# Second modulation on turned tiles, first normalizations on VectorE, twelve row places, another order for the last tiles

## Chip, cores, metric

One NeuronCore of a Trainium2 chip runs the whole kernel in one launch. The metric is the device time of an execution in microseconds. Each figure of the profile comes from one profiled execution.

## What is computed

Two batches of 2048 tokens, 128 channels. `mod` gives six vectors of 128 per batch. The first half is a gated linear recurrence, the second a mixture of eight experts of which each token takes two.

```python
sa, ca, ga, sb, cb, gb = (mod[:, 0], mod[:, 1], mod[:, 2], mod[:, 3], mod[:, 4], mod[:, 5])
h = _layernorm(x, axis=-1) * (1 + ca) + sa
x = x + ga * _L0_attn_ref(h, ...)      # two sigmoid gates, a = exp(log_a), y = scan(a, b)
h = _layernorm(x, axis=-1) * (1 + cb) + sb
x = x + gb * _L0_ffn_ref(h, ...)
# ffn: logits = silu(x @ rw1 + rb1) @ rw2 + rb2; top 2 of 8, softmax;
#      out += we[:, None] * (silu(x @ w1[e] + b1[e]) @ w2[e] + b2[e])
```

## The kernel before

The 4096 tokens are eight groups of 512 (four tiles of 128 rows); groups 0 to 3 are batch 0, 4 to 7 batch 1. Everything is float32.

For each group g, in the names of the order lists: `stats1` (mean and variance, VectorE), `rstd1` (GpSimd, power -0.5), `norm1` (GpSimd for groups 0 to 2, VectorE for the rest), `turn_x` (TensorE turns rows to channels), `modulate` (ScalarE, 1 + ca and sa as per-partition scale and bias), `gates` (TensorE), `tanh`, `decay` (exp), `clamp`, `mult` (sqrt) on ScalarE, `input` and `scan` on VectorE, `turn_y` back, `resid` (adds x, statistics of the second norm), `rstd2` on GpSimd for groups 0 to 3 or `root` on VectorE for 4 to 7, and `norm2`: eight instructions that subtract the mean, multiply by 1 + cb, multiply by rs and add sb, with cb and sb spread over all partitions by `modrow` and `rowsA`. Then `turn_h`, `copy` (ScalarE), four `router` products with four `silu`, `logits`, `lgc`, `sum`, `top2`, `share`, `rank` and `place`, which gives each token's two slots in DRAM.

`send` (GpSimd): 64 indirect DMAs, eight for each group, write the normalized rows with weight and target row to `sorted_rows`, each expert's rows together. They wait for `place` of the group and for a doubling DMA that SP issues after `norm2`. Each expert's rows end in a padding block, written by eight DMAs of SP once `late_table` has given the offsets (`pad_i`).

The expert stage works through 39 tiles of 256 rows of one expert. `early_table` (after group 3 has its slots) lists the first nine tiles, all of batch 0; `late_table` and `table_row` (after group 7) the other 30. Per tile: SP loads the rows (`xr`), TensorE turns them (`tx`, bank 1), VectorE copies them out (`xT`) and copies the expert's first weights to a pair of buffers (`w1`), TensorE runs layer1 (`l1`), ScalarE `hid` (silu), VectorE `w2`, TensorE layer2 (`l2`, bank 7), ScalarE `yb`, TensorE turns back (`ty`, bank 1), VectorE scales (`sc`), GpSimd scatters two halves to `expert_out` (`scat`). `tx` and `ty` share bank 1 in a fixed turn. Rows and results have ten places each (`U`), so the load of tile s waits for the scatter of tile s - 10.

Up to tile 10 every engine follows its list in `PLAN` (instructions joined with + alternate); then come a loop over 20 tiles (`ROUNDS * U`) and a static rest with `step`. In the rest, `SUMS` says in which step VectorE adds the two expert results of a group (`combine`, three instructions). SP's queue in order: input loads, eight doublings, nine tile loads (after `s_tab` 1 and the sends of batch 0), eight paddings, tile loads from 9 on (after `s_tab` 2, padding, all sends), loads of results, stores. At the end four DMAs of SP fetch group 7's results in halves. `keep_warm` issues eleven matmuls of ident beside the first small products.

## Time and profile before

| | |
|---|---|
| time, median of 3 runs | 288.79 us (288.6 to 292.12) |
| profiled execution | 288.09 us, span 286.2 us |
| TensorE busy | 248.1 us, 87% |
| VectorE busy | 188.4 us, 66% |
| ScalarE busy | 166.5 us, 58% |
| GpSimd busy | 171.6 us, 60% |
| mean granted TensorE clock | 0.956 |

The span runs from the first to the last instruction. Engines are PE (TensorE; PEld its weight loads), DVE (VectorE), ACT (ScalarE), POOL (GpSimd) and SP; SPq is the queue on which SP issues DMAs. L1205 is line 1205 of the kernel. In a timeline row the bracket gives the idle time ahead of the instruction and what ended it. A float32 matmul shows as two records.

### The profile page before, as it was taken

The page shows a single profiled execution, that of the slowest core. Times are in us where ns is not written, and L with a number is a line of the kernel's source. Part 1 is how long each engine was busy: PE and PEld are TensorE (multiplying, and loading weights), DVE is VectorE, ACT ScalarE, POOL GpSimd, SP SyncE. Part 2 cuts the span into 40 slices and gives each one's busy share as a digit, 9 for nine tenths or more (in the row PEclk, how much of TensorE's full clock was granted, in tenths as well). Part 3 has the DMA queues.
Part 4 walks back from the last instruction along what each step waited for, and adds up shares of the span by engine and source line. Part 5 has one row for each costly group of instructions (what it writes and reads, how often), then busy time and mean ns, then how long its engine had stood idle before and what let it go on. Part 6 is the DMA issues. An engine that isn't in the chain of part 4 may idle for free.

```text
span 286.2 us, 4950 instructions
## 1 busy us (share of the span) xinstructions
PE 248.1 (87%) x1179; PEld 178.0 (62%) x1179; DVE 188.4 (66%) x750; ACT 166.5 (58%) x322; POOL 171.6 (60%) x192
## 2 busy tenths in 40 slices
PE   7767759997599798999999999999999999989910
PEld 6424334444144245687878888888888888868700
DVE  3959999999999987576444444444444446866533
ACT  4189979999785355545555555555555556445300
POOL 4996211267777757777777777644554445645650
PEclk9997979999779799999999999999999999999995
DMA  7993011121131226413533333222217822280505
GB/s 222 308 333 117 19 40 38 37 75 50 55 121 48 89 82 157 114 47 115 149 84 85 111 101 109 57 75 75 74 46 214 221 72 74 84 256 4 161 0 147
DMA packets 45365, 30.51 MB, mean 107 GB/s; under 512 B 5085, under 2 KB 41999, under 8 KB 45342
## 3 DMA queue, kind: packets, MB, share of 16 engines
q1 hardware_dynamic: 40432, 21.75, 27.9%
q0 software_dynamic: 4544, 8.47, 9.0%
q8 instruction: 8, 0.13, 0.2%
q14 instruction: 15, 0.12, 0.2%
q10 hardware_dynamic: 366, 0.04, 0.1%
HBM read 16.39 MB, written 12.67 MB: 102 GB/s over the span
## 4 chain that ended last, share of the span: by engine, by line
PE 40%; POOL 27%; issue 14%; DVE 12%; DMA 4%; POOLq 1%; DVEq 0%; SPq 0%; ACT 0%
POOL sorted_rows L550 21%; PE bank L1218 18%; PE bank L1205 18%; POOL shared L514 3%; PE bank L1226 3%; PE bank L1194 2%; DVE st L698 2%; DMA expert_out<-shared,tx 2%; POOL rs L506 1%; DVE shared L718 1%; POOL expert_out L559 1%; DVE tx L792 1%; DMA xs<-in_L_attn_x_dram 1%; DVE xs L803 1%; DMA tx<-sorted_rows 1%
## 5 line engine op out<-in xcount | busy, mean ns | idle before, releaser
L559 POOL DMA_INDIRECT expert_out<-shared,tx x78 | 80.4, 1031 | 52.9 <-DVE shared L1012 37.4
L657 ACT ACTIVATE hT<-bank,w_t 128x256 f32<-128x256 f32 x156 | 65.4, 470 | 29.3 <-PE bank L1205 28.3
L550 POOL DMA_INDIRECT sorted_rows<-rows,sloti x64 | 63.9, 999 | 27.2 <-issue 18.3
L1205 PE MATMUL bank<-xT,w_t 128*128 128x256 f32 x312 | 74.1, 380 | 0.1
L1218 PE MATMUL bank<-hT,w_t 128*128 128x256 f32 x312 | 74.1, 380 | 0.0
L1205 PEld LDWEIGHTS bank<-xT,w_t 128*128 128x128 f32 x312 | 56.3, 190 | 6.8 <-DVE w_t L995 0.7
L1218 PEld LDWEIGHTS bank<-hT,w_t 128*128 128x128 f32 x312 | 56.2, 190 | 6.2
L666 ACT ACTIVATE yT<-bank,w_t 128x256 f32<-128x256 f32 x39 | 18.4, 473 | 47.6 <-PE bank L1218 47.6
L1134 PE MATMUL bank<-h2T,rw_s 128*128 128x512 f32 x64 | 36.8, 677 | 1.7 <-ACT qv L644 1.4
L986 DVE COPY xT<-bank 128x256 f32<-128x256 f32 x39 | 16.5, 422 | 23.6 <-PE bank L1194 23.6
L1012 DVE TENSOR_TENSOR shared<-bank,tx 128x256 f32<-128x256 f32 x39 | 16.5, 423 | 21.3 <-PE bank L1226 21.2
L995 DVE COPY w_t<-w_s 128x516 f32 x39 | 17.2, 442 | 16.7 <-issue 15.9
L1004 DVE COPY w_t<-w_s 128x513 f32 x39 | 17.3, 443 | 15.3 <-issue 14.4
L1134 PEld LDWEIGHTS bank<-h2T,rw_s 128*128 128x128 f32 x64 | 10.8, 205 | 14.4 <-issue 5.9
L698 DVE BATCH_NORM_STATS2 st<-xs 128x6 f32<-128x128 f32 x64 | 15.7, 282 | 4.2 <-DMA xs<-in_L_attn_x_dram 4.1
L1226 PE MATMUL bank<-ident,yT 128*128 128x128 f32 x78 | 15.2, 276 | 2.5 <-ACT yT L666 1.1
L1194 PE MATMUL bank<-ident,tx 128*128 128x128 f32 x78 | 15.2, 276 | 1.8 <-DMA tx<-sorted_rows 1.3
L1226 PEld LDWEIGHTS bank<-ident,yT 128*128 128x128 f32 x78 | 10.3, 141 | 8.3 <-issue 3.3
L1194 PEld LDWEIGHTS bank<-ident,tx 128*128 128x128 f32 x78 | 10.4, 141 | 7.7 <-DMA tx<-sorted_rows 2.3
L644 ACT ACTIVATE qv<-bank,smallbT 128x512 f32<-128x512 f32 x16 | 10.8, 686 | 6.3 <-PE bank L1134 6.2
L506 POOL TENSOR_TENSOR rs<-ve,half_neg 128x4 f32<-128x4 f32 x8 | 9.3, 1164 | 8.0 <-DVE ve L705 8.0
L542 POOL TENSOR_TENSOR rs<-ve,half_neg 128x4 f32<-128x4 f32 x4 | 4.1, 1035 | 15.7 <-DVE ve L705 15.7
(194 smaller groups left out, 328.9 us busy)
## 6 DMA issues: line engine op xcount, KB each, us to landing
tx<-sorted_rows SPq DMA_DIRECT2D x39, 130.0 KB, 2.2
w_s<-in_L_ffn_w_dram SPq DMA_DIRECT2D x16, 256.0 KB, 6.1
xs<-in_L_attn_x_dram SPq DMA_DIRECT2D x8, 256.0 KB, 5.2
rows<-rows SPq DMA_DIRECT2D x8, 256.0 KB, 2.6
av<-expert_out SPq DMA_DIRECT2D x8, 256.0 KB, 3.7
qv<-expert_out SPq DMA_DIRECT2D x6, 256.0 KB, 5.0
expert_out<-shared,tx POOLq DMA_INDIRECT x78, 2.3
sorted_rows<-padr SPq DMA_DIRECT2D x9, 130.0 KB, 3.0
```

Source lines behind the costliest of these rows:

```text
L550: p.indirect_dma_start(sorted_rows[:, :], bass.IndirectOffsetOnAxis(ap=sloti[:, k, t:t + 1], axis=0), rows[:, t, k, :], None).then_inc(s_d ...
L559: p.indirect_dma_start(expert_out[:, :], bass.IndirectOffsetOnAxis(ap=xr_i[:, s % U, n, D + 1:D + 2], axis=0), yo[:, s % U, n, :], None, b ...
L657: ins = nc.scalar.activation(hsT[:, u % 2, h, :], bank[4 + q][:, (h % 2) * SL:(h % 2 + 1) * SL], ACT.Silu, bias=w1_t[:, u % 2, HID + h:HID ...
L666: nc.scalar.activation(yT[:, u % 2, :], bank[7][:, 0:SL], ACT.Identity, bias=w2_t[:, u % 2, HC * D:W2E]).then_inc(s_yT_e, 1)
L698: ins = v.bn_stats(st[:, t, :], xs[:, t, :])
L995: v.tensor_copy(w1_t[:, u % 2, :], w1_s[:, bass.ds(e * WE, WE)]).then_inc(s_w1t, 1)
L1004: v.tensor_copy(w2_t[:, u % 2, :], w2_s[:, bass.ds(e * W2E, W2E)]).then_inc(s_w2t, 1)
L1134: t.matmul(bank[2 + n % 2][:, :], rw1_s[:, h * P:(h + 1) * P], h2T[:, g % 2, :], start=True, stop=True).then_inc(s_rl1, 1)
L1194: ins = t.transpose(bank[1][:, n * P:(n + 1) * P], xr[:, u, n, 0:D], ident[:, :])
L1205: ins = t.matmul(bank[4 + h // 2][:, (h % 2) * SL:(h % 2 + 1) * SL], w1_t[:, u % 2, h * P:(h + 1) * P], xT[:, u % 2, :], start=True, stop= ...
L1218: ins = t.matmul(bank[7][:, 0:SL], w2_t[:, u % 2, h * D:(h + 1) * D], hsT[:, u % 2, h, :], start=(h == 0), stop=(h == HC - 1))
L1226: ins = t.transpose(bank[1][:, n * P:(n + 1) * P], yT[:, u % 2, n * P:(n + 1) * P], ident[:, :])
```

## The change

- `norm2` only subtracts the mean and multiplies by rs (four instructions). 1 + cb and sb are applied after the turn, where they are per-partition values: for the router in `copy` on ScalarE, for the experts in `take_x`. `mod2` and `mods2` compute these columns; `modrow` and `rowsA` keep only gb.
- A tile from 9 on can hold rows of both batches. A third row of the table gives its split; `take_x` then writes all columns with batch 0's values and after that the columns from the split on with batch 1's.
- `w2` moves from VectorE to ScalarE. `norm1` is VectorE's for all groups. `keep_warm` is gone.
- Rows and results have twelve places; tiles 0 and 1 use places 10 and 11, and the lists go up to tile 11.
- The last tiles: layer2 of 37 has bank 2 and stands ahead of layer1 of 38, and the last bias, turn, scale and scatter go by halves. Group 7's result loads are issued half by SP, half by ScalarE.
- All lists are in another order.

```diff
     U = 10
-    FIRST = 11
+    FIRST = 12
+    SLOTS = 12
-    POOLED = 3
             "tensor": """
+                turnc:0 mod:0 turn_x:0 mod2:0 gates:0 turn_x:1 turn_x:2 gates:1 gates:2 turn_x:3 turn_x:4 gates:3
+                turn_x:5 turn_y:0 gates:4 turnb:0 turn_y:1 gates:5 modrow:0 turn_h:0 turn_x:6 router:0 turn_h:1
+                router:1 turn_y:2 gates:6 router:2 router:3 router:4 turn_y:3 logits:0 router:5 router:6 sum:0
+                turn_h:2 turn_x:7 router:7 rank:0 router:8 turn_y:4 router:9 logits:1 router:10 router:11 turn_h:3
+                sum:1 logits:2 rank:1 sum:2 router:12 turn_h:4 router:13 gates:7 router:14 rank:2 turn_y:5 router:15
+                turn_y:6 router:16 logits:3 router:17 sum:3 turn_h:5 router:18 router:19 rank:3 router:20 logits:4
+                turn_h:6 count:0 sum:4 router:21 turn_y:7 router:22 router:23 router:24 rank:4 router:25 router:26
+                logits:5 router:27 turn_h:7 sum:5 logits:6 router:28 router:29 rank:5 router:30 router:31 tx:0 sum:6
+                tx:1 l1:0 tx:2 logits:7 rank:6 l1:1 l2:0 tx:3 l1:2 sum:7 ty:0 lev:0 l2:1 tx:4 l1:3 ty:1 l2:2 rank:7
+                tx:5 l1:4 ty:2 l2:3 tx:6 count:1 l1:5 ty:3 l2:4 tx:7 l1:6 ty:4 l2:5 tturn:0 tx:8 l1:7 ty:5 l2:6 l1:8
+                ty:6 l2:7 tx:9 tx:10 l1:9 ty:7 l2:8 tx:11 l1:10 ty:8 l2:9 tx:12 l1:11 ty:9 l2:10""",
             "vector": """
...
-                norm2:4 place:2 norm2:5 scan:6 scan:7+top2:3 resid:6 place:3 resid:7+root:6 norm2:6 top2:4+root:7
...
-                w1:2 xT:2 xT:3 w1:3 w2:1 rowsB:0 sc:0 w2:2 top2:7 xT:4 w1:4 place:7 w2:3 sc:1 w1:5 xT:5 w2:4 table2:0
-                sc:2 w1:6 xT:6 sc:3 xT:7 w2:5 w1:7 w2:6 sc:4 w2:7 xT:8 table3:0 sc:5 w1:8 w1:9 sc:6 w2:8 xT:9 w2:9
-                w1:10 xT:10 sc:7 xT:11 w1:11 sc:8 w2:10""",
+                stats1:0 setup:0 stats1:1+norm1:0 stats1:2+mods:0 norm1:1+soft:0 norm1:2 stats1:3 input:0 stats1:4
+                norm1:3+stats1:5 csilb:0 norm1:4 input:1 mods2:0 norm1:5 scan:0 scan:1 stats1:6 input:2
+                resid:0+stats1:7 resid:1 input:3 colsb:0 norm2:0 norm2:1 norm1:6 scan:2 scan:3 resid:2+consts:0
+                input:4 scan:4+rowsA:0 norm2:2 resid:3+norm1:7 top2:0 place:0 norm2:3 resid:4 root:4 norm2:4 top2:1
+                place:1 input:5 input:6 top2:2 scan:5 scan:6 resid:5+place:2 resid:6+root:5 norm2:5 top2:3+root:6
+                norm2:6 input:7 place:3 scan:7 table1:0+top2:4 resid:7 root:7 norm2:7 place:4 top2:5 w1:0 place:5 xT:0
+                xT:1 top2:6 w1:1 xT:2 w1:2 place:6 w1:3 xT:3 table1b:0 sc:0 xT:4 top2:7 w1:4 sc:1 xT:5 w1:5 place:7
+                sc:2 w1:6 xT:6 table1c:0 sc:3 w1:7 xT:7 table2:0+rowsB:0 sc:4 w1:8 xT:8 table3:0 w1:9 sc:5 sc:6 xT:9
+                xT:10 sc:7 w1:10 w1:11 xT:11 sc:8 xT:12 w1:12 sc:9""",
...
-                hid:4 yb:3 hid:5 yb:4 hid:6 yb:5 hid:7 yb:6 hid:8 yb:7 hid:9 yb:8 hid:10""",
+                csil:0 esp:0 modulate:0 tanh:0 modulate:1 decay:0 modulate:2 clamp:0 tanh:1 decay:1 mult:0 clamp:1
+                modulate:3 mult:1 tanh:2 modulate:4 tanh:3 decay:2 modulate:5 clamp:2 tanh:4 decay:3 decay:4 tanh:5
+                mult:2 copy:0 clamp:3 mult:3 modulate:6 clamp:4 mult:4 silu:0 silu:1 copy:1 silu:2 silu:3 silu:4
+                decay:5 lgc:0 silu:5 silu:6 copy:2 share:0 silu:7 tanh:6 modulate:7 clamp:5 silu:8 silu:9 lgc:1
+                silu:10 silu:11 decay:6 lgc:2 share:1 copy:3 clamp:6 mult:5 mult:6 silu:12 copy:4 silu:13 share:2
+                silu:14 tanh:7 silu:15 decay:7 lgc:3 silu:16 clamp:7 silu:17 copy:5 silu:18 share:3 silu:19 mult:7
+                lgc:4 silu:20 silu:21 copy:6 silu:22 silu:23 silu:24 share:4 silu:25 lgc:5 silu:26 silu:27 copy:7
+                silu:28 share:5 lgc:6 silu:29 silu:30 silu:31 hid:0 w2:0 share:6 hid:1 w2:1 yb:0 lgc:7 w2:2 hid:2 yb:1
...
+        def out_bank(s):
+            return bank[2] if static(s) and s == TILES - 2 else bank[7]
         SUMS = {FIRST + ROUNDS * U: 0, FIRST + ROUNDS * U + 1: 1, FIRST + ROUNDS * U + 2: 2,
-                FIRST + ROUNDS * U + 3: 3, MID + 13: 4, FIVE + 6: 5, TILES + 1: 6}
+                FIRST + ROUNDS * U + 3: 3, FIRST + ROUNDS * U + 4: 4, TILES - 1: 5, TILES + 1: 6}
...
-            return (s - u) // U + 1
+            if static(s) and s < SLOTS:
+                return 1
+            return (s - u) // U + 1 if u >= SLOTS - U else (s - u - U) // U + 1
...
+        def slot(s):
+            return U + s if s < SLOTS - U else s % U
...
+        def load_last(eng, k):
+            for half, done in ((0, s_y01[NG - 1]), (1, s_y7b)):
+                at = k * TOK + (NG - 1) * G + half * G // 2
+                eng.dma_start(y01[NG - 1][:, k, 2 * half:2 * half + 2, :], expert_out[at:at + G // 2, :]
+                              .rearrange("(n p) d -> p n d", p=P)).then_inc(done, 16)
...
-                if not (static(s) and s < U):
+                if not (static(s) and s < SLOTS):
...
-                if s * HALVES * ROW + HALVES * ROW > GPB * G and s * HALVES * ROW <= GPB * G:
+                if s == 0:
...
-            def ln1_norm(g):
-                pool.wait_ge(s_rstd1, g + 1)
...
-                for j in range(GT):
-                    t = g * GT + j
-                    ins = p.tensor_scalar(xn[:, g % 2, j, :], xs[:, t, :], mv1[:, t, 0:1], rs1[:, t:t + 1],
-                                          ALU.subtract, ALU.mult)
-                ins.then_inc(s_xnp, 1)
...
                 for n in range(HALVES):
+                    if s == TILES - 1 and n:
+                        pool.wait_ge(s_yo, s + 1 + n)
...
-                nc.scalar.copy(h2T[:, g % 2, :], turn_bank("turn_h", g)[:, :]).then_inc(s_h2T, 1)
+                if g == 0:
+                    act.wait_ge(s_modok, 2)
+                b = g // GPB
+                nc.scalar.activation(h2T[:, g % 2, :], turn_bank("turn_h", g)[:, :], ACT.Identity,
+                                     bias=modc[:, 3, b:b + 1], scale=gac[:, 3, b:b + 1]).then_inc(s_h2T, 1)
...
+            def weights2(s, u):
+                if static(s) and s == 0:
+                    act.wait_ge(s_tab, 1)
+                if static(s) and s == EARLY:
+                    act.wait_ge(s_tab, 2)
+                e = act.value_load(tab[0:1, 1, bass.ds(s, 1)], min_val=0, max_val=NE - 1)
+                if static(s) and s == 0:
+                    act.wait_ge(s_w2, 16 * NE)
+                    act.wait_ge(s_constd, 1)
+                if not (static(s) and s < 2):
+                    act.wait_ge(s_yT_e, s - 1)
+                nc.scalar.copy(w2_t[:, u % 2, :], w2_s[:, bass.ds(e * W2E, W2E)]).then_inc(s_w2t, 1)
...
+            def bias_last(s, u):
+                act.wait_ge(s_l2, s + 1)
+                act.wait_ge(s_yturn, s - 1)
+                for n in range(HALVES):
+                    nc.scalar.activation(yT[:, u % 2, n * P:(n + 1) * P], out_bank(s)[:, n * P:(n + 1) * P],
+                                         ACT.Identity, bias=w2_t[:, u % 2, HC * D:W2E]).then_inc(s_yT_e, 1)
             def step(s, u):
+                if static(s) and s >= TILES - 1:
+                    if s == TILES - 1:
+                        bias_out(s - 2, step_slot(s, u, -2))
+                        weights2(s, u)
+                        bias_out(s - 1, step_slot(s, u, -1))
+                        hidden(s, u)
+                        bias_last(s, u)
+                    return
...
                     hidden(s, u)
+                    weights2(s, u)
...
+            landed(act, TILES - 1)
+            load_last(act, 1)
...
+            def mod_columns2(_):
+                dve.wait_ge(s_modc, 2)
+                yield from link(v.tensor_copy(modc[:, 3:5, :], bank[6][:, 3 * B:5 * B].rearrange("p (i b) -> p i b", b=B)))
+                v.tensor_scalar(gac[:, 3, :], modc[:, 4, :], 1.0, None, ALU.add).then_inc(s_modok, 1)
...
             def ln2_norm(g):
-                b = g // GPB
                 for j in range(GT):
                     t = g * GT + j
-                    ins = v.scalar_tensor_tensor(rows[:, t, 0, 0:D], xs[:, t, :], mv2[:, t, 0:1], cbB[:, b, :],
-                                                 ALU.subtract, ALU.mult)
-                    if j < GT - 1:
-                        yield
-                yield from link(ins)
-                for j in range(GT):
-                    t = g * GT + j
-                    ins = v.scalar_tensor_tensor(rows[:, t, 0, 0:D], rows[:, t, 0, 0:D], rs2[:, t:t + 1],
-                                                 sbB[:, b, :], ALU.mult, ALU.add)
+                    ins = v.tensor_scalar(rows[:, t, 0, 0:D], xs[:, t, :], mv2[:, t, 0:1], rs2[:, t:t + 1],
+                                          ALU.subtract, ALU.mult)
...
                 for b in range(B):
                     m = bank[6 + b]
-                    v.tensor_copy(sbB[:, b, :], m[:, 0:D])
+                    v.tensor_scalar(gbS[:, b, :], m[:, 0:D], 0.0, 2.0, ALU.is_ge, ALU.mult)
                     yield
-                    v.tensor_scalar(cbB[:, b, :], m[:, D:2 * D], 1.0, None, ALU.add)
-                    yield
-                    v.tensor_scalar(gbS[:, b, :], m[:, 2 * D:3 * D], 0.0, 2.0, ALU.is_ge, ALU.mult)
-                    yield
-                    ins = v.tensor_copy(gbB[:, b, :], m[:, 2 * D:3 * D])
+                    ins = v.tensor_copy(gbB[:, b, :], m[:, 0:D])
...
+                by_level = val2[:, 2, :].rearrange("p (l e) -> p l e", l=LEVELS)
+                v.tensor_copy(row_0[:, 2:3], first[:, 0:1])
...
                 dve.wait_ge(s_tturn, 1)
-                v.tensor_scalar(tab[:, :, EARLY:TILES], table_bank().rearrange("p (k s) -> p k s", k=2),
-                                float(NE * REG), None, ALU.min).then_inc(s_tab, 1)
+                turned = table_bank().rearrange("p (k s) -> p k s", k=3)
+                v.tensor_scalar(tab[:, 0:2, EARLY:TILES], turned[:, 0:2, :], float(NE * REG), None, ALU.min)
+                v.tensor_copy(split[:, :], turned[:, 2, :]).then_inc(s_split, 1)
+                dve.wait_ge(s_split, 1)
+                v.tensor_tensor(split[:, :], split[:, :], turned[:, 0, :], ALU.subtract).then_inc(s_split, 1)
+                dve.wait_ge(s_split, 2)
+                v.tensor_scalar(tab[:, 2, EARLY:TILES], split[:, :], 0.0, float(SL), ALU.max, ALU.min).then_inc(s_tab, 1)
                 dve.wait_ge(s_tab, 2)
             def expert_of(s):
                 return dve.value_load(tab[0:1, 1, bass.ds(s, 1)], min_val=0, max_val=NE - 1)
             def take_x(s, u):
+                early = static(s) and s < EARLY
+                if not early:
+                    k = dve.value_load(tab[0:1, 2, bass.ds(s, 1)], min_val=0, max_val=SL)
                 dve.wait_ge(s_txp, s + 1)
                 if not (static(s) and s < 2):
                     dve.wait_ge(s_l1, 2 * (s - 1))
-                v.tensor_copy(xT[:, u % 2, :], bank[1][:, 0:SL]).then_inc(s_xT, 1)
+                if static(s) and s == 0:
+                    dve.wait_ge(s_modok, 2)
+                v.tensor_scalar(xT[:, u % 2, 0:SL], bank[1][:, 0:SL], gac[:, 3, 0:1], modc[:, 3, 0:1],
+                                ALU.mult, ALU.add).then_inc(s_xT if early else s_xa, 1)
+                if not early:
+                    dve.wait_ge(s_xa, s - EARLY + 1)
+                    v.tensor_scalar(xT[:, u % 2, bass.ds(k, SL)], bank[1][:, bass.ds(k, SL)], gac[:, 3, 1:2],
+                                    modc[:, 3, 1:2], ALU.mult, ALU.add).then_inc(s_xT, 1)
...
-            def weights2(s, u):
-                e = expert_of(s)
...
+            def scale_last(s, u):
+                for n in range(HALVES):
+                    dve.wait_ge(s_yturn, s + 1 + n)
+                    v.tensor_tensor(yo[:, u, n, :], bank[1 - n][:, 0:P], xr[:, u, n, D:D + 1].to_broadcast([P, D]),
+                                    ALU.mult).then_inc(s_yo, 1)
...
-            def keep_warm(n):
-                if n == 0:
-                    pe.wait_ge(s_ident, 1)
-                for _ in range((4, 4, 3)[n]):
-                    t.matmul(bank[4][:, 0:P], ident[:, :], ident[:, :], start=True, stop=True)
...
+            def modulation2(_):
+                pe.wait_ge(s_modok, 1)
+                for i in range(3, 5):
+                    ins = t.matmul(bank[6][:, i * B:(i + 1) * B], wmod_s[:, i * D:(i + 1) * D], csil[:, :],
+                                   start=True, stop=True)
+                ins.then_inc(s_modc, 1)
...
-                    ins = t.matmul(bank[6 + b][:, 0:3 * D], csil_b[:, b, :], wmod_s[:, 3 * D:6 * D],
-                                   start=True, stop=True)
+                    ins = t.matmul(bank[6 + b][:, 0:D], csil_b[:, b, :], wmod_s[:, 5 * D:6 * D], start=True, stop=True)
...
             def xn_transpose(g):
-                if g < POOLED:
-                    pe.wait_ge(s_xnp, g + 1)
-                else:
-                    pe.wait_ge(s_xn, g - POOLED + 1)
+                pe.wait_ge(s_xn, g + 1)
...
+            def layer2(s, u, between=None):
                 pe.wait_ge(s_w2t, s + 1)
-                pe.wait_ge(s_hs, 2 * (s + 1))
+                if not (static(s) and s == TILES - 1):
+                    pe.wait_ge(s_hs, 2 * (s + 1))
                 if static(s) and s < 1:
                     pe.wait_ge(s_tab, 1)
+                elif static(s) and s >= TILES - 2:
+                    pe.wait_ge(s_yT_e, TILES - 2 if s == TILES - 1 else TILES - 3)
                 else:
                     pe.wait_ge(s_yT_e, s)
                 for h in range(HC):
-                    ins = t.matmul(bank[7][:, 0:SL], w2_t[:, u % 2, h * D:(h + 1) * D], hsT[:, u % 2, h, :],
+                    if static(s) and s == TILES - 1 and h % 2 == 0:
+                        pe.wait_ge(s_hs, 2 * s + h // 2 + 1)
+                    ins = t.matmul(out_bank(s)[:, 0:SL], w2_t[:, u % 2, h * D:(h + 1) * D], hsT[:, u % 2, h, :],
                                    start=(h == 0), stop=(h == HC - 1))
+                    if h == 1 and between:
+                        between()
                 ins.then_inc(s_l2, 1)
...
+            def turn_last(s, u):
+                for n in range(HALVES):
+                    pe.wait_ge(s_yT_e, s + 1 + n)
+                    if n == 0:
+                        wait_tile_bank(pe, "ty", s)
+                    t.transpose(bank[1 - n][:, 0:P], yT[:, u % 2, n * P:(n + 1) * P], ident[:, :]).then_inc(s_yturn, 1)
...
+                if static(s) and s >= TILES - 1:
+                    if s == TILES - 1:
+                        layer2(s - 1, step_slot(s, u, -1), lambda: turn_out(s - 2, step_slot(s, u, -2)))
+                        layer1(s, u)
+                        turn_out(s - 1, step_slot(s, u, -1))
+                        layer2(s, u)
+                        turn_last(s, u)
+                    return
```

## Rows read from the trace of the kernel before

**Rows 1.** The page's 40 slices of 7.155 us, busy tenths: TensorE, VectorE, ScalarE.
```profile
PE   7767759997599798999999999999999999989910
DVE  3959999999999987576444444444444446866533
ACT  4189979999785355545555555555555556445300
```
**Rows 2.** The chain of waits, 143 to 155 us: start, us, what.
```profile
143.89 1.00 POOL expert_out L559
...
148.28 2.31 DMA tx<-sorted_rows
...
151.07 1.73 PE bank L1205 x8
...
154.97 1.73 PE bank L1205 x8
```
**Rows 3.** Stretches: length, then each engine's busy us, granted clock, DMA share, GB/s.
```profile
34.00:38.70 4.70, 0.00 (x0) 0.00 (x0) 4.67 (x21) 4.06 (x6) 0.46 (x1) 1.00 0.00 0
38.70:43.00 4.30, 4.27 (x12) 2.62 (x13) 4.23 (x6) 3.39 (x5) 0.58 (x1) 0.60 0.24 67
...
151.00:266.00 115.00, 113.79 (x580) 97.58 (x579) 58.50 (x132) 61.86 (x144) 67.11 (x66) 1.00 0.37 103
```
**Rows 4.** VectorE's timeline: a first normalization, and the padding offsets.
```profile
20.47 1.11 DVE L718 TENSOR_SCALAR shared<-xs,mv,rs 128x128 f32<-128x128 f32 x4 [2.47 <-POOL rs L506]
...
131.10 0.14 DVE L960 CAST pad_i<-bank 1x8 int32<-1x8 f32 x1
```
**Rows 5.** Groups of instructions, VectorE: busy us, mean ns, idle before.
```profile
L1004 DVE COPY w_t<-w_s 128x513 f32 x39 | 17.3, 443 | 15.3 <-issue 14.4 <-ACT yT L666 0.9
...
L986 DVE COPY xT<-bank 128x256 f32<-128x256 f32 x39 | 16.5, 422 | 23.6 <-PE bank L1194 23.6
...
L823 DVE SCALAR_TENSOR_TENSOR rows<-rows,rs,sbB 128x128 f32<-128x128 f32 x32 | 9.4, 343 | 0.2
...
L718 DVE TENSOR_SCALAR shared<-xs,mv,rs 128x128 f32<-128x128 f32 x20 | 5.9, 335 | 2.5 <-POOL rs L506 2.5
```
**Rows 6.** ScalarE's timeline at a change of tables.
```profile
22.39 1.28 ACT L620 ACT_TABLE_LOAD   x1
23.68 0.63 ACT L620 ACTIVATE qv<-qv 128x512 f32<-128x512 f32 x1
```
**Rows 7.** TensorE's timeline: first gate, tile 0's layer1, tile 7's row turn.
```profile
11.46 2.05 PE L1110 MATMUL bank<-hT,wx_bd 128*128 128x512 f32 x2 [0.96 <-ACT hT L592]
...
111.48 1.97 PE L1205 MATMUL bank<-xT,w_t 128*128 128x256 f32 x8
...
137.47 0.38 PE L1194 MATMUL bank<-ident,tx 128*128 128x128 f32 x2
```
**Rows 8.** GpSimd's timeline: sends 1, 32 and 64.
```profile
58.18 1.38 POOL L550 DMA_INDIRECT sorted_rows<-rows,sloti  x1 [5.73 <-DVE sloti L864]
...
99.86 0.96 POOL L550 DMA_INDIRECT sorted_rows<-rows,sloti  x1 [0.31 <-issue]
...
142.63 0.96 POOL L550 DMA_INDIRECT sorted_rows<-rows,sloti  x1 [0.31 <-issue]
```
**Rows 9.** SP's timeline, 99 to 148 us: start, us of issuing, queue.
```profile
106.08 10.05 SPq L411 DMA_DIRECT2D tx<-sorted_rows  x9
132.01 8.39 SPq L400 DMA_DIRECT2D sorted_rows<-padr  x8
145.72 0.39 SPq L411 DMA_DIRECT2D tx<-sorted_rows  x1
```
**Rows 10.** The page's DMA issues: KB each, median us to landing.
```profile
sorted_rows<-padr SPq DMA_DIRECT2D x9, 130.0 KB, 3.0
```
**Rows 11.** Timeline of the tail: PE's weight load of tile 37's turn, SP's last loads.
```profile
270.37 0.20 PEld L1226 LDWEIGHTS bank<-ident,yT 128*128 128x128 f32 x2 [0.97 <-ACT yT L666]
...
278.19 1.91 SPq L465 DMA_DIRECT2D qv<-expert_out  x4
```

158 lines of the change are left out of this document (67 added, 91 removed).

## Prediction

> **What bounds the kernel now.** I read the page's slices first [rows 1]. From slice 2 to 14 (7 to 107 us) VectorE stands at 8 or 9 and PE mostly at 5 to 9; from slice 17 on PE stands at 9 and VectorE at 4 to 6. Next the chain of waits [rows 2]: before it comes to these rows it runs through GpSimd's 64 indirect sends, one after the other; then come the scatter of tile 0, its landing, the load of tile 10, and from 151.07 us layers of TensorE back to back, 3.90 us from one tile's first layer to the next tile's. A stretch view confirms it: 113.8 of the 115 us from 151 to 266 are PE's, while VectorE is 51% and ScalarE 54% busy [rows 3]. So three things set the end: how early the tile stage starts, what holds it at tiles 9 and 10 (the first that need all sends), and the tail.
>
> **The start, up to the first send.** VectorE's order up to place:0 is nearly a sum of its own work; after the gap that ends at 20.47 [rows 4] it has none worth naming until the first send's slots are ready near 57.8. Ahead of place:0 the change adds three first normalizations (L718 at 335 ns, overlapping, four in 1.03: 3.1 in all), scan:4 (two instructions, 1.9) and mods2 (two tiny ones, 0.35). It takes off input:5 (0.6), half of rowsA (four instructions of 0.2, 0.8), and L823 [rows 5], the second instruction of norm2, for groups 0 to 2. Four L823 fill 1.15 us alone, but two of the three sets stand between statistics and partly fill gaps: 0.66 + 0.66 + 1.2 = 2.5. Less interleaving costs some 0.6. Net +2.0. Against this stands the gap of 2.47 us at 20.47 [rows 4], where VectorE waited for rs of group 3 because GpSimd, itself normalizing three groups, came late to it; it goes, and a wait of 0.4 for the biases with it. place:0 ends near 57.0: first send 57.3 instead of 58.18, 0.9 earlier.
>
> The cover for this is ScalarE. Counted through its new order it switches tables 15 times instead of 13, once more ahead of share:0 (silu:4, decay:5, silu:5). A switch costs 1.28 us, and the next ACTIVATE starts 0.01 us behind it [rows 6]. By the same durations lgc:0 ends at 52.3, the sums at 53.3, and top2:0 wants them at 53.9: hidden, with 0.6 us to spare. The Trainium skill (ScalarE: Activation LUTs, What ACT_TABLE_LOAD costs) puts a switch at about 2.66 us, a drain included. No such gap stands in these rows, so the measured 1.28 is used; by the page, an estimate, the later table switches would push place:0 some 2 us back and the total to 287.9.
>
> The warm-up matmuls go. They bought nothing: gates:0 still runs at 2.05 us for two records from 11.46 [rows 7], twice the 1.02 of the same pair later, with the warm-up ahead of it. I charge zero. The Trainium skill (TensorE: Matmul & The Clock Gate, Part 1) says that activity ahead releases the half rate, which speaks for keeping them; had it been so here, taking them away could have cost up to 1.9 us of the first gates.
>
> **The sends and tile 0.** 31 intervals from 58.18 to 99.86 make 41.7 us [rows 8]. About 0.5 of that are waits for place:1 and place:2, which now come before their turn: 41.2, so the 32nd send starts at 98.5. The last send starts at 142.63 and the load that waits for all is issued at 145.72, 3.1 us on [rows 8, 9]. The same step puts tile 0's load at 101.6, against 106.08 now [rows 9]. Today it does not wait for sends but for table1 and a register load on SP. In the new order table1 stands before resid:7, root:7 and norm2:7 and ends near 92; norm2:7 ends near 98.5, as five more normalizations are halved (5 x 1.15). place:4 comes at 99.1, which takes most of a hole of 2.1 us ahead of the 33rd send: last send 57.3 + 84.45 - 2.3 = 139.4, seen at 142.5. Layer1:0 starts 5.4 us after its load now (111.48 [rows 7, 9]) and 5.0 then: 106.6.
>
> **What is late next: the padding.** Eight padding DMAs stand on SP's queue ahead of tile 9's load and wait for late_table's pad_i. Now: pad_i 131.10 [rows 4], issues from 132.01 for 8.4 us [rows 9], the last at 140.0, landed a median 3.0 later [rows 10]: 143.0, covered by the sends. The new order holds table2 back behind xT:7. PE from layer1:0 to tx:7: eleven layers of 1.73 (19.0), nine pairs of transposes of 0.22 (2.0), logits:7 and sum:7 (1.8), ranks and counts (0.7), small stalls (0.7): 24.2; the same stretch takes 26.0 now, with router:31 in it (111.48 to 137.47 [rows 7]). So tx:7 at 130.8, pad_i 131.4, first padding +0.9, last +8.0, landed +3.0, register load and issue +0.7: tile 9 is loaded at 144.0, tile 10 at 145.1 (one issue in 1.1 us: nine in 10.05 [rows 9]), it lands 2.3 later [rows 2], and layer1:9 starts at 147.9. Twelve row places do what they are for: tile 10 no longer waits for scatter 0 (143.89 to 148.3 [rows 2]). Today layer1:9 starts at 151.07 in the chain: 3.2 earlier. Bounds: 4.7 if the sends alone decide, 1.0 if table2 slips half a tile.
>
> **The clock after the wait.** PE is through with layer2:7 near 142.4 and then has nothing until 146.3. PE stood still from 34.0 to 38.7, and was then granted a mean 0.60 of its clock until 43, partly 1.2 GHz, partly 2.4 [rows 3]: 0.40 x 4.3 = 1.7 us lost. After a wait of this length I take 1.8; nothing covers it, PE is the bound from there on. Bounds 0 and 2.2. Of the 3.2, 1.4 are left.
>
> **The tile stage.** Per tile VectorE loses the w2 copy (L1004, 0.44) and gains the second column copy (as L986, 0.42, and a short wait for its own first) [rows 5]; a register load goes and one comes. xT is ready 0.5 later, inside layer1's 1.73. ScalarE gains a copy of 513 columns, 0.6 to 0.8 as its forms with 512, and a register load: 3.4 of 3.90 us, hidden. h2T with scale and bias costs up to 0.2 more than as a copy, beside PE. The sums of groups 0 to 4 (2.06 us each on VectorE) now stand in five steps in a row, where VectorE needs 4.4 of 3.90; today such steps cost some 2 us in all. I add 0.3 (0 to 2).
>
> **The tail.** Today the last output transposition but one waits 0.97 us for yT of tile 37, and layer2:38 stands behind it [rows 11]. In the new order layer2:37, in a bank of its own, runs ahead of layer1:38, and layer2:38 follows it with only the second half of hidden to wait for: it ends 0.8 earlier. Half-wide bias, turn and scale bring the scatters 0.4 more forward. The four last loads are issued in turn from 278.19 within 1.91 us [rows 11]; on two queues the first half is complete 0.45 sooner. -1.65 in all (1.0 to 2.2).
>
> **Sum.** -1.4 + 0.3 - 1.65 = -2.75 against the profiled execution's 288.09 us (span 286.2 and 1.9 around it): 285.3. The median of the three runs, 288.79, lies 0.7 above that execution; I say 285.9. 2% of 288.79 (283.0 to 294.6) is about what a measurement of this kernel can tell from no change.
>
> **Rivals.** *The clock holds, or the wait is short* (stalls spread over tiles 0 to 8, or the sends decide): the 1.8 isn't charged and up to 1.5 more comes, 282.6 to 284.3. For it: the order was relieved at both ends; against: the one wait of that length was followed by 0.60 [rows 3]. *ScalarE becomes the bound of the start* (the slower one): place:0, all sends and tile 0 hang one for one on lgc:0, which has 0.6 us of slack. One more late switch and two silus behind it (1.28 + 1.3) make 2.6. The kernel is slower than before once the first send comes after 60.0; at 61.5 it takes 290. For it: ScalarE stands at 7 to 9 in slices 4 to 11; against: at 5 thereafter, so it could catch up [rows 1]. *The two-pass copy and the later table eat the lead*: table2 slips by a tile, the padding lands at 147, layer1:9 starts near 151 and the clock still dips: 287 to 288.8, no change.
>
> **Chances.** Forecast as summed 0.43 (284.5 to 287), clock holds 0.27, table late 0.15, ScalarE bound 0.15. The range leaves out the ends of the first rival and of the slower one: 282.7 to 289.8. Faster than 283.0: 0.17, the better half of the second case and a bit beyond; slower than 294.6: 0.03; within 2%: 0.80.
>
> **What would show it.** First send at 57.3; tile 0's load at 101.6; pad_i near 131.4; tile 9's load right behind the padding's landing, not behind the last send; a hole of some 4 us on PE near 144 and a granted clock near 0.6 after it; then 3.90 us a tile again; from the last layer to the end 12.9 us instead of 13.7. Wrong it is if the first send moves by more than 2 us either way, if PE's hole is under 2 us, or if the steps with sums take over 4.5 us.

## The result, and the profile after

On the chip where both were first timed the changed kernel takes 293.52 us (median of 6, 292.63 to 294.75) and the kernel before 290.51 (median of 6, 288.6 to 292.24): ratio 1.013, 95% interval 1.0085 to 1.0175. That is slower, by 0.85 to 1.75%, and outside the predicted range of 282.7 to 289.8; it stays within the 2% (283.0 to 294.6) that the prediction called no change. A ratio counts, on both sides, only the executions within 1.5% of the fastest of their kernel. The profiled execution takes 292.63 us, span 290.8, mean granted clock 0.935; before it was 288.09, 286.2 and 0.956. The six times of the kernel before fall at 288.6 to 288.9 and at 292.1 to 292.2, and its profile is of a short one: the profiles differ by 4.5 us, the medians by 3.0.

The page's slices (7.27 us each; TensorE, VectorE, ScalarE) answer to [rows 1]: ScalarE has mostly risen by a tenth or two in the tile stage, and TensorE's row has 9 from slice 14 to 35, but for the 3 of slice 20 (145 to 153 us): there TensorE stands still.

```profile
PE   2877679797969899999939999999999999998920
...
DVE  3999987999997946467414355444445554988533
ACT  4199996999978645666633676666676766666500
```

The chain of waits answers to [rows 2]; each line: start, us, what.

```profile
136.04 0.07 DVE pad_i L1003
...
144.25 0.37 SPq L419
...
145.54 2.17 DMA sorted_rows<-padr
...
148.48 2.08 DMA tx<-sorted_rows
...
151.93 0.56 DVE xT L1043
...
153.28 3.41 PE bank L1257 x8
```

GpSimd's sends are gone from this part. In their place stand pad_i, the eight paddings, their landing, the load of tile 9, its turn, and the second pass of its copy. Then tile 9's layer1 takes 3.41 us, twice its usual time. The timelines of GpSimd and SP, which answer to [rows 8] and [rows 9]:

```profile
58.80 1.29 POOL L555 DMA_INDIRECT sorted_rows<-rows,sloti  x1 [1.89 <-DVE sloti L904]
...
142.03 0.95 POOL L555 DMA_INDIRECT sorted_rows<-rows,sloti  x1 [0.30 <-issue]
```

```profile
101.93 0.59 SPq L441 DMA_DIRECT2D rows<-rows  x1
104.06 10.34 SPq L430 DMA_DIRECT2D tx<-sorted_rows  x9
136.84 9.07 SPq L419 DMA_DIRECT2D sorted_rows<-padr  x8
148.48 9.40 SPq L430 DMA_DIRECT2D tx<-sorted_rows  x6
```

The last send starts 0.6 us earlier than before, the padding 4.8 later, and tile 9's load 2.8 later. TensorE's timeline, which answers to [rows 7]: first layer of tile 0, row turn of tile 7, row turns of tiles 9 and 10.

```profile
110.06 1.89 PE L1257 MATMUL bank<-xT,w_t 128*128 128x256 f32 x8
...
135.07 0.38 PE L1246 MATMUL bank<-ident,tx 128*128 128x128 f32 x2
...
150.61 0.56 PE L1246 MATMUL bank<-ident,tx 128*128 128x128 f32 x2 [3.60 <-DMA tx<-sorted_rows]
152.62 0.66 PE L1246 MATMUL bank<-ident,tx 128*128 128x128 f32 x2 [1.45 <-DVE xT L1043]
```

The stretches, which answer to [rows 3]: TensorE has nothing for 3.6 us, is then granted 0.59 of its clock for 8.4 us (a mix of 1.2 and 2.4 GHz), and is full from 159 on.

```profile
147.00:150.60 3.60, 0.02 (x1) 0.00 (x0) 0.00 (x0) 1.71 (x3) 2.82 (x3) 1.00 0.32 92
150.60:159.00 8.40, 6.94 (x23) 5.47 (x24) 3.35 (x7) 1.68 (x4) 6.26 (x8) 0.59 0.46 123
159.00:247.00 88.00, 88.00 (x453) 76.19 (x452) 41.81 (x91) 59.96 (x135) 47.17 (x48) 1.00 0.35 96
```

The costliest groups of the page, which answer to [rows 5]: the copy out of PSUM with a per-partition scale and bias takes 543 ns where the plain one took 422, and each late tile has two of them.

```profile
L1039 DVE TENSOR_SCALAR xT<-bank,gac,modc 128x256 f32<-128x256 f32 x39 | 21.2, 543 | 47.8 <-PE bank L1246 47.1
...
L1043 DVE TENSOR_SCALAR xT<-bank,gac,modc x30 | 16.3, 544 | 4.8 <-DVE xT L1039 2.6
```

The tail, which answers to [rows 11]: the turn of tile 35's output waits for the second pass of xT of tile 38; then ScalarE's yT of tile 36, the scale and the scatters of tile 38, the last loads on two queues.

```profile
269.34 0.41 PE L1285 MATMUL bank<-ident,yT 128*128 128x128 f32 x2 [0.90 <-DVE xT L1043]
...
271.51 0.47 ACT L690 ACTIVATE yT<-bank,w_t 128x256 f32<-128x256 f32 x1 [1.69 <-PE bank L1275]
...
278.10 0.55 DVE L1088 TENSOR_TENSOR shared<-bank,tx 128x128 f32<-128x128 f32 x2 [2.27 <-PE bank L1301]
...
278.81 1.29 POOL L566 DMA_INDIRECT expert_out<-shared,tx  x1 [0.30 <-DVE shared L1088]
...
280.41 1.15 POOL L566 DMA_INDIRECT expert_out<-shared,tx  x1 [0.30 <-issue]
282.96 0.88 SPq L398 DMA_DIRECT2D qv<-expert_out  x2
283.02 0.95 ACTq L398 DMA_DIRECT2D qv<-expert_out  x2
```

Three marks split the difference: ScalarE's first yT of tile 10 (162.65 us before, 167.09 after), that of tile 36 (266.17, 271.51), and the span's end (286.2, 290.8). So **+4.44 up to tile 10, +0.90 from there to tile 36, -0.74 in the tail**: +4.6, which is the difference of the two profiled executions. I use these marks for the experiments too: "stage" is tile 10 to tile 36 (103.52 before, 104.42 after), "end" is tile 36 to the end (20.03, 19.29), "entry" is the start of tile 9's row turn to yT of tile 10 (13.25 before, 149.40 to 162.65; 16.48 after, 150.61 to 167.09).

### The profile page after: what moved, and what is told of

Its sections match the earlier page's. It is cut to its first block, busy times and chain, and to the rows that moved or that the text cites. A ratio compares the mean times of both kernels' runs of the same rounds, so it can differ in the third digit from the quotient of the medians.

```text
span 290.8 us, 5105 instructions
## 1 busy us (share of the span) xinstructions
PE 247.5 (85%) x1162; PEld 178.7 (61%) x1162; DVE 186.7 (64%) x727; ACT 191.4 (66%) x365; POOL 161.3 (55%) x180
## 4 chain that ended last, share of the span: by engine, by line
PE 48%; DVE 33%; issue 5%; DMA 5%; SPq 3%; DVEq 2%; POOL 1%; ACT 1%; POOLq 0%; ACTq 0%
PE bank L1275 17%; PE bank L1257 17%; PE bank L1186 4%; DVE st L740 4%; DVE shared L760 3%; PE bank L1246 3%; DVE rows L863 3%; PE bank L1113 2%; PE bank L1285 2%; DVE xT L1039 2%; DVE mv L745 2%; DVE xs L851 2%; POOL expert_out L566 1%; DMA xs<-in_L_attn_x_dram 1%; SPq L451 1%
## 5 line engine op out<-in xcount | busy, mean ns | idle before, releaser
L566 POOL DMA_INDIRECT expert_out<-shared,tx x78 | 79.5, 1020 | 59.0 <-DVE shared L1061 44.1
L1257 PE MATMUL bank<-xT,w_t 128*128 128x256 f32 x312 | 75.7, 387 | 0.7 <-DVE w_t L1053 0.7
L1257 PEld LDWEIGHTS bank<-xT,w_t 128*128 128x128 f32 x312 | 57.6, 194 | 7.2 <-DVE w_t L1053 0.8
L1275 PEld LDWEIGHTS bank<-hT,w_t 128*128 128x128 f32 x312 | 56.7, 192 | 6.3
L1039 DVE TENSOR_SCALAR xT<-bank,gac,modc 128x256 f32<-128x256 f32 x39 | 21.2, 543 | 47.8 <-PE bank L1246 47.1
L1186 PE MATMUL bank<-h2T,rw_s 128*128 128x512 f32 x64 | 38.5, 708 | 0.2
L684 ACT COPY w_t<-w_s 128x513 f32 x39 | 24.2, 620 | 2.2 <-ACT yT L690 1.0
L1061 DVE TENSOR_TENSOR shared<-bank,tx 128x256 f32<-128x256 f32 x38 | 15.9, 419 | 9.5 <-PE bank L1285 8.6
L1043 DVE TENSOR_SCALAR xT<-bank,gac,modc x30 | 16.3, 544 | 4.8 <-DVE xT L1039 2.6
L1186 PEld LDWEIGHTS bank<-h2T,rw_s 128*128 128x128 f32 x64 | 11.7, 216 | 12.0 <-issue 7.4
```

The costliest lines, as they stand in the source:

```text
L566: p.indirect_dma_start(expert_out[:, :], bass.IndirectOffsetOnAxis(ap=xr_i[:, slot(s), n, D + 1:D + 2], axis=0), yo[:, slot(s), n, :], Non ...
L684: nc.scalar.copy(w2_t[:, u % 2, :], w2_s[:, bass.ds(e * W2E, W2E)]).then_inc(s_w2t, 1)
L1039: v.tensor_scalar(xT[:, u % 2, 0:SL], bank[1][:, 0:SL], gac[:, 3, 0:1], modc[:, 3, 0:1], ALU.mult, ALU.add).then_inc(s_xT if early else s_ ...
L1186: t.matmul(bank[2 + n % 2][:, :], rw1_s[:, h * P:(h + 1) * P], h2T[:, g % 2, :], start=True, stop=True).then_inc(s_rl1, 1)
L1257: ins = t.matmul(bank[4 + h // 2][:, (h % 2) * SL:(h % 2 + 1) * SL], w1_t[:, u % 2, h * P:(h + 1) * P], xT[:, u % 2, 0:SL], start=True, st ...
L1275: ins = t.matmul(out_bank(s)[:, 0:SL], w2_t[:, u % 2, h * D:(h + 1) * D], hsT[:, u % 2, h, :], start=(h == 0), stop=(h == HC - 1))
```

## Experiments

Sixteen kernels in four groups; each group ran on one chip beside the kernel before. The first group's chip gave the kernel before 289.8 us, like the first. The other three gave it 330.8, 332.3 and 332.2 us: there, between 60 and 190 us, engines stop now and then for 2 to 12 us, put down to nothing in the kernel, which no row of the first chip shows. Times of those groups are compared within the group only, and lengths of stretches outside these stalls with the first chip's: the stage of the changed kernel is 104.36 to 104.47 us in its two profiles there and 104.42 on chip one. A longer one of 104.84 in kernel 6 shows how far a single profile can be off.

**1. The table early** (chip one).

```diff
-  ... table1b:0 sc:0 xT:4 ... xT:6 table1c:0 sc:3 w1:7 xT:7 table2:0+rowsB:0 sc:4
+  ... table1b:0 sc:0 table1c:0 xT:4 ... xT:6 table2:0+rowsB:0 sc:3 w1:7 xT:7 sc:4
```

> The changed kernel with table1c right behind sc:0 and table2 right behind xT:6, nothing else. Padding theory (the late table alone makes the hole and with it the dip of the clock): pad_i comes near 131.9 instead of 135.95, the last padding lands some 4 us earlier than now, tile 9 is loaded right behind the landing of the last send at about 145.7 instead of 148.48, TensorE waits about 1 us for it instead of 3.6, its clock stays at 1.00, and layer1:10 starts 4 to 5 us earlier (159.2 to about 154.5): 4.0 to 4.9 us off the changed kernel's time, ratio to the kernel before 0.996 to 1.000. Rival 1 (the clock falls anyway, since the wait is only shortened): 2.7 us off, ratio near 1.004. Rival 2 (the sends or the scatters hold tiles 9 and 10 in any case): under 1 us off, ratio 1.010 or more.

Measured: ratio 0.9989 (0.9952 to 1.0025), against 1.013 for the changed kernel: 1.4%, 4.1 us. SP's and TensorE's timelines:

```profile
101.47 10.56 SPq L430 DMA_DIRECT2D tx<-sorted_rows  x9
131.51 8.48 SPq L419 DMA_DIRECT2D sorted_rows<-padr  x8
144.14 14.55 SPq L430 DMA_DIRECT2D tx<-sorted_rows  x7
...
146.40 0.44 PE L1246 MATMUL bank<-ident,tx 128*128 128x128 f32 x2 [0.69 <-DMA tx<-sorted_rows]
...
148.53 1.89 PE L1257 MATMUL bank<-xT,w_t 128*128 128x256 f32 x8
```

The padding is 5.3 us earlier, 2.1 of it by an earlier first send and 3.3 by the table. Tile 9's load is no longer behind it but behind the landing of the last send (139.59 to 143.34): the row turn of tile 9 waits 0.69 us, and tile 9's layer1 takes its 1.89. Entry is 14.26 us instead of 16.48. Padding theory held. This profiled execution is the shortest of twelve (286.2 us, median 289.88) and had a luckier start, which the next view shows: the changed kernel's own start, here without a half clock. The stretches of this kernel:

```profile
39.00:46.00 7.00, 6.12 (x23) 3.29 (x24) 6.93 (x36) 6.91 (x10) 0.00 (x0) 1.00 0.20 61
144.00:149.00 5.00, 2.87 (x15) 2.06 (x15) 1.77 (x4) 2.36 (x5) 3.78 (x5) 1.00 0.51 132
```

and the same first stretch of the changed kernel:

```profile
39.00:46.00 7.00, 7.00 (x19) 4.24 (x20) 4.58 (x8) 6.43 (x9) 0.00 (x0) 0.57 0.14 43
```

TensorE's and VectorE's timelines in it, first the changed kernel, then this one (both have the same order here):

```profile
39.85 1.92 PE L1186 MATMUL bank<-h2T,rw_s 128*128 128x512 f32 x2
...
44.12 1.03 PE L1113 MATMUL bank<-ident,hT 128*128 128x128 f32 x4
...
45.18 0.69 DVE L851 TENSOR_TENSOR xs<-bank,xs 128x512 f32<-128x512 f32 x1 [2.35 <-PE bank L1113]
```

```profile
39.83 1.02 PE L1186 MATMUL bank<-h2T,rw_s 128*128 128x512 f32 x2
...
41.99 0.60 PE L1113 MATMUL bank<-ident,hT 128*128 128x128 f32 x4
...
43.15 0.67 DVE L851 TENSOR_TENSOR xs<-bank,xs 128x512 f32<-128x512 f32 x1
```

At half clock the two router products and the turn ahead of turn_y:2 take 1.92, 1.91 and 1.03 us instead of 1.02, 1.02 and 0.60, and VectorE waits 2.35 us for it. The first send starts at 56.73 here and at 58.80 in the changed kernel; tile 0 is loaded at 101.47 here, where I had put 101.6.

**2. One copy of xT.** The second pass and its register load are left out: rows of batch 1 from tile 9 on get batch 0's modulation.

```diff
-                if not early:
-                    dve.wait_ge(s_xa, s - EARLY + 1)
-                    v.tensor_scalar(xT[:, u % 2, bass.ds(k, SL)], bank[1][:, bass.ds(k, SL)], ...
```

> The changed kernel with one copy of xT for every tile: leaves out the second pass over the columns that belong to batch 1 (rows of batch 1 from tile 9 on get the modulation of batch 0) and its register load. If the second pass costs what its two places show: tx:10 starts 0.7 us earlier in the hole of tile 9, and in the steps with sums of groups VectorE's work falls by 0.7 us to near 3.7 of 3.9 us, so that the five steps of 4.34 to 4.5 go back to about 3.9: together 2.5 to 3.5 us off the changed kernel, ratio to the kernel before 1.001 to 1.005. If it is hidden as I priced it (0.3 in all): ratio 1.010 or more, steps with sums unchanged.

Measured: ratio 0.9923 (0.9878 to 0.9968). In the profile 3.8 us less than the changed kernel: stage 101.18 instead of 104.42, entry 15.81 instead of 16.48 with the hole (4.16 us) and the half clock still there. The five steps with sums are 3.9 us each instead of 4.34, 4.37, 4.33, 4.54 and 4.98. The second pass isn't hidden. The ratio's 2% is more than the 3.8 us. Two of the twelve executions (285.2 and 285.7 us) ran at a mean clock of 0.95 and 0.956 instead of 0.934 and weigh in it; the median of all twelve, 289.22, lies 4.3 us below the changed kernel's.

**3. turn_y:2 ahead of router:0** on TensorE, the order that makes VectorE wait.

```diff
- turn_x:6 router:0 turn_h:1 router:1 turn_y:2 gates:6
+ turn_x:6 turn_y:2 router:0 turn_h:1 router:1 gates:6
```

> The changed kernel with turn_y:2 ahead of router:0 on TensorE instead of behind router:1, nothing else. If TensorE's order at half clock is what makes VectorE wait 2.35 us at 42.8: that wait falls to under 0.5 us, the first send starts near 57.0 instead of 58.80, and as VectorE has hardly a gap from there to norm2:7, tile 0's load and layer1:0 come 1 to 1.8 us earlier; the end follows by 0.5 to 1.5 us (hole and dip remain, since pad_i hangs on the same stretch), ratio to the kernel before 1.007 to 1.011. Rival: ScalarE's chain to lgc:0 (53.82, then sum:0, top2:0) is next at once, as router:0 comes later by the length of turn_y:2: first send not before 57.9 and tile 0's load moves under 0.5 us, ratio 1.012 to 1.014.

Measured: ratio 1.0129 (1.0088 to 1.0171), no gain. VectorE's wait at 42.8 is gone, but ScalarE's table load ahead of silu:0 starts at 44.05 instead of 42.19, lgc:0 ends 1.73 us later, and the first send comes at 59.92. The rival held: both orders are tied, in profiles with a granted clock of 0.57 and 0.59 from 39 to 46 us.

**4. First normalizations of groups 0 to 2 on GpSimd again**, in the new order.

```diff
- stats1:1+norm1:0 stats1:2+mods:0 norm1:1+soft:0 norm1:2 stats1:3
+ stats1:1 stats1:2+mods:0 soft:0 stats1:3          (and norm1:0 to 2 behind their rstd1 on GpSimd)
```

> The changed kernel with the first normalizations of groups 0 to 2 on GpSimd again, each behind its rstd1, and the rest of every order as changed. My step (VectorE loses 3.1 us of work, but waits 2.47 us for rs of group 3 as the kernel before did): the first send moves by under 1 us either way and the time stays within 1 us of the changed kernel. Rival (VectorE has no slack, and the moved normalizations are what ate the gain of the halved second ones): first send 1.5 us or more earlier, time 1 to 2 us less.

Measured: ratio 1.0267 (1.023 to 1.0305), first send at 62.12. Neither held. TensorE's row turns at 9.59 and 19.54 wait 2.64 and 3.26 us for GpSimd's normalizations, and VectorE 3.99 us at 22.7 for its rs. Having the normalizations on VectorE is worth some 4 us in the order that the change gives, where I had set 3.1 us of added work against a gap of 2.47; the other lists have given up the slack that GpSimd's pace needs.

**5 and 6. Fillers on TensorE** (chip with stalls): 28 idle matmuls ahead of tx:9; 12 behind gates:5 and 10 behind turn_h:0. Neither the changed kernel nor kernel 1 ran on this chip, so the ratios of 5 to 7 say nothing against theirs.

```diff
+                for _ in range((28, 12, 10)[n]):
+                    t.matmul(bank[3 if n == 0 else 2][:, 0:P], ident[:, :], ident[:, :], start=True, stop=True)
```

> The changed kernel with 28 extra 128-column matmuls into an unused bank on TensorE between layer2:7 and the transposition of tile 9, so that TensorE is busy in most of the 3.6 us in which it waited for tile 9. Nothing is left out; 3.0 us of useless work are added where TensorE had nothing to do. If standing still is what brings the dip: granted clock near 1.00 from 150.6 to 159 instead of 0.59, layer1:9 takes 1.89 us instead of 3.62, layer1:10 comes about 2.2 us earlier with tile 9's load unmoved; time 2 to 2.5 us below the changed kernel, ratio to the kernel before 1.004 to 1.007. Rival (the clock falls at that point whatever TensorE does, as it does five times in this kernel): no gain, ratio 1.012 or more.

> The changed kernel with 12 extra 128-column matmuls on TensorE behind gates:5 and 10 behind turn_h:0 (34 to 39 us, where TensorE is 2.07 of 5 us busy). If low activity there is what halves the clock from 39 to 46 (0.57 in the changed kernel's profile, 1.00 in the profile of the kernel with the earlier table, which sent first at 56.73 and not at 58.80): granted clock 1.00 in that stretch, VectorE's wait of 2.35 us for turn_y:2 gone, first send near 56.8, tile 0's load near 101.6, and pad_i 2 us earlier; time 1.5 to 2.5 us below the changed kernel, ratio 1.004 to 1.008. Rival (the dip falls where it likes, or moves to the next stretch): first send anywhere from 56.7 to 59, ratio 1.010 to 1.015.

Measured: 1.0145 (1.0083 to 1.0208) and 0.9949 (0.9908 to 0.999). I had the filler's size wrong: 28 took 6.42 us, 0.23 each. Behind it the clock is 1.00 and layer1:9 takes 1.89, but tile 9 had landed 4.7 us before the filler's end; without it the hole would have been 1.5 us (an estimate: TensorE free at 188.81, load issued at 188.16 and landing 2.2 later). In the second the clock is 1.00 from 39 to 46 us where the first has 0.76, and the first send comes at 57.38 instead of 58.24: the direction held. In two later kernels with the same filler it comes at 57.67 and 58.28, against 57.23 in their control at 0.79. The clock is 1.00 in all three kernels with the filler and in two of the eleven profiles without it that have the same lists up to there; that the filler gains time isn't shown.

**7. A bank for the turned rows** (with the early table): from tile 9 on they go to bank 3, and `ty` waits only for the scale before it.

```diff
+        def x_bank(s):
+            return bank[1] if static(s) and s < EARLY else bank[3]
```

> The kernel with the earlier table, and the transposed rows of tiles 9 and up in a bank of their own (3), so that the output's transposition of a step waits no longer for both passes of xT of the next tile. If the 3.2 us that the second pass costs from the first yT of tile 10 to that of tile 36 (104.42 us with it, 101.18 without) come from the one bank that two transpositions share: that stretch falls to 101.5 to 102.2 us, the five steps with sums to 3.9 to 4.1 us, tx:10 starts right behind tx:9; 2.3 to 3.3 us below the kernel with the earlier table, ratio to the kernel before 0.988 to 0.992. Rival (VectorE's 4.4 us of work in a step with a sum are the bound, whatever bank): the steps stay at 4.3 and only the 0.9 us at step 36 and 1.0 us at tile 10 go, ratio 0.993 to 0.996.

Measured: 0.9945 (0.9907 to 0.9984). The steps with sums are 3.9 us as hoped, stage 101.75, but end is 21.08 instead of 19.3. GpSimd's timeline:

```profile
307.89 0.98 POOL L567 DMA_INDIRECT expert_out<-shared,tx  x1 [2.07 <-DVE shared L1062]
...
310.47 1.07 POOL L567 DMA_INDIRECT expert_out<-shared,tx  x1 [0.30 <-issue]
...
317.47 0.98 POOL L567 DMA_INDIRECT expert_out<-shared,tx  x1 [0.30 <-issue]
```

VectorE needs 4.3 to 4.6 us in a step with a sum and falls behind; the output scales come late, and of the last eight scatters (307.89 to 317.47) the seven behind the first follow each other without a wait. Of the 2.7 us that the stage gains 1.8 are handed to the tail.

**8. Twelve row places alone**, in the kernel before.

```diff
-    FIRST = 11
+    FIRST = 12
+    SLOTS = 12
```

> The kernel before with twelve row places and twelve static steps instead of ten and eleven, nothing else: with it the load of tile 10 waits no longer for the scatter of tile 0. My step: it does what it is for, and alone it is worth only the 0.85 us that the transposition of tile 10 waited for its rows (tile 9's rows come as before): 0.5 to 0.9 us, ratio 0.997 to 0.998. Rival (the whole 3.2 us that I booked for the first tile behind all sends come from here): ratio under 0.993. Other rival (the sums of the first groups start one step later and cost in the tail): ratio 1.000 or more.

Measured: 0.9994 (0.9946 to 1.0042), no difference that this can show. With the places comes another step for the sums of groups 0 to 3, one later, so that five steps with sums stand in a row as in the changed kernel: stage is 104.36 us here against 103.52 before, entry 12.99 against 13.25, end 20.15 against 20.03. The rival of the later sums is seen in the stage, with 0.84 us.

**9 to 12. Control, short filler, combinations** (another chip with stalls). The control is the changed kernel itself.

> The changed kernel once more, as the control that runs on the same chip as the three others: ratio to the kernel before 1.010 to 1.015 as in its own measurement, tile 9's load some 2.7 us behind where the last send's landing would allow it, granted clock about 0.6 from 150.6 to 159.

> The changed kernel with 14 extra 128-column matmuls between layer2:7 and the transposition of tile 9 instead of 28 (28 took 6.42 us and held tile 9 up by some 4.5 us beyond the landing of its rows; 14 take 3.2, less than the wait of 3.6). Standing still as the cause of the dip: clock 1.00 from 150.6 on, layer1:9 in 1.89 us, layer1:10 about 2.2 us earlier relative to tile 9's load, time 2 us below the control. Rival (the 28 kept the clock by their length, and a shorter filler with a gap of 0.4 us and the waits of tile 10 behind it doesn't): layer1:9 at 3.6 us again and the time of the control.

> Earlier table, 12 and 10 filler matmuls at the start (34 to 39 us), and a bank of its own for the transposed rows from tile 9 on. If the three prices add: hole and dip (3.8 us), the half clock of the start in the executions that have it (1.4 us), and 0.9 us from the bank (2.7 us of the stage less 1.8 us that the scatters queue up in the tail): 5 to 6 us below the control, ratio to the kernel before 0.992 to 0.996 and below. Rival (the gains overlap, since an earlier start meets the same last send): 3.8 to 4.5 us below the control, ratio 0.997 to 0.999.

> The same without the bank: earlier table and the filler at the start only. 4 to 5 us below the control; against the one with the bank it tells what the bank is worth in all: 0.9 us if the tail takes back what the stage gains, 2.7 us if the tail's queue of scatters was that chip's alone.

Measured, in this order: control 0.9833 (0.9755 to 0.9912), where I had expected 1.010 to 1.015 (its six executions run from 324.2 to 332.5 us; the medians give 0.992); short filler 0.9955 (0.9913 to 0.9998); early table, start filler and bank 0.9795 (0.9744 to 0.9845); the same without the bank 0.985 (0.9802 to 0.9898). The control has no hole: tile 7 is so late by stalls that tile 9 is there in time, so the filler had nothing to fill and cost its 3.29 us. The control and the two combinations can't be told apart (medians 329.6, 326.7 and 327.0 us).

**13 to 16. Once more** (a third chip with stalls): control, a kernel with early table, bank and the sum of group 4 in step 37, the old tail, the short filler.

> The changed kernel, control for the other three. On a chip without the stalls that hit all engines: ratio 1.010 to 1.015, hole of 3.6 us and granted clock 0.6 behind it. On one with them: ratio 0.983 to 0.995 and no hole.

> Earlier table, a bank of its own for the transposed rows from tile 9 on, and the sum of group 4 in step 37 instead of 36. If VectorE's lag is what the tail inherits: first yT of tile 10 to that of tile 36 in 101.2 to 101.8 us, from there to the end 19.3 to 19.8 us instead of the 21.1 with five sums in a row, the last eight scatters no longer back to back; 2.3 to 2.9 us less than the kernel with the earlier table alone. On a chip without the stalls ratio to the kernel before 0.985 to 0.991. Rival (the lag of four sums is enough to queue the scatters up): 20.5 to 21 us from tile 36 to the end, 1 us less only.

> The changed kernel with the last steps as before: one output bank, whole yT and whole scale for tile 38, layer2:37 behind layer1:38, all four last loads on SyncE. By the rows of the changed kernel the new tail gives 0.7 us from the first yT of tile 36 to the end (19.3 against 20.03): this kernel then takes 20.0 us there, and its time is 0.5 to 0.9 us above the control's. By my prediction's term it would be 20.9 and 1.65 above. Rival (the new order only moves work from tile 38 to 37): the stretch from the first yT of tile 35 to the end is the same in both.

> The changed kernel with 14 extra matmuls of 0.23 us between layer2:7 and the transposition of tile 9. If there is a hole in the control: clock at 1.00 behind it, layer1:9 in 1.89 us instead of 3.62, tile 9's load to layer1:10 in 8.5 us instead of 10.7, time 2.0 to 2.5 us below the control. Rival (the clock falls at this point of time whatever TensorE does): same clock, same time as the control. Where the control has no hole, the filler costs up to its 3.2 us, and the question stays open.

Measured: control 0.9815 (0.9792 to 0.9839), second kernel 0.9789 (0.9741 to 0.9837), old tail 0.9818 (0.9777 to 0.9859), short filler 0.9895 (0.9855 to 0.9935). The first three intervals overlap: neither the second kernel's gain nor the new tail's shows in the times. In the profiles stage and end of the second are 101.87 and 20.18 us, 1.65 less in sum than the control's 104.36 and 19.34: the moved sum gives back 0.8 of what the tail took. With the old tail the end is 20.44, 1.10 more than with the new. The control's profile, of a long execution this time (335.35 us, median 326.37), has a hole of 2.49 us, between the 0 and 3.6 of the others:

```profile
180.83 0.66 PE L1246 MATMUL bank<-ident,tx 128*128 128x128 f32 x2 [9.18 <-DVE shared L1061]
181.28 3.62 PE L1257 MATMUL bank<-xT,w_t 128*128 128x256 f32 x8
...
194.34 0.44 PE L1246 MATMUL bank<-ident,tx 128*128 128x128 f32 x2 [2.49 <-DMA tx<-sorted_rows]
...
196.68 3.15 PE L1257 MATMUL bank<-xT,w_t 128*128 128x256 f32 x8
```

Its entry is 15.56 us. So entry goes with the hole: 14.04 and 14.06 where there was none, 14.26 with 0.69 us, 14.14 with 1.20 (kernel 6), 15.56 with 2.49, 16.48 with 3.60, 15.99 and 16.51 with 3.95 and 4.04 (kernels 3 and 4). A wait of 3.6 us costs 2.2 to 2.4 us more in clock. The rival of kernels 5 and 16, that the clock falls at this point of time whatever TensorE does, is answered by the first two lines and their like: in all twelve profiles of the chips with stalls TensorE stands for 3.70 to 11.96 us ahead of tile 8's row turn, between 169.7 and 181.0 us, and the layer1 behind it takes 3.36 to 3.62 us instead of 1.89. Whether a filler would save the clock stays open: kernels 10 and 16 had none to fill, and kernel 5 only 1.5 us.

**Why the sign is another on the chips with stalls** stays open. Rows of the control on the second of them, ScalarE's, TensorE's and SP's timelines:

```profile
94.50 0.78 ACT L636 ACTIVATE h2T<-bank,modc,gac 128x512 f32<-128x512 f32 x1 [6.88 <-remote]
...
169.70 0.66 PE L1246 MATMUL bank<-ident,tx 128*128 128x128 f32 x2 [8.52 <-issue]
...
113.81 19.25 SPq L430 DMA_DIRECT2D tx<-sorted_rows  x9
```

Where an engine's stop is put down to nothing in the kernel (remote, issue), and the nine loads take 19.25 us to issue instead of 10.34, the order of the tables may matter less; that isn't shown. The kernel before, unedited, has no profile from such a chip. The nearest is kernel 8, whose time is the same: its yT of tile 10 starts at 205.59 us, 42.9 later than on chip one before, while in kernels 9 and 15 it starts at 199.46 and 198.68, 32.4 and 31.6 later than in the changed kernel on chip one. Behind tile 10 the three have the stage of chip one (104.36, 104.47 and 104.38 us). So what the changed kernel wins there it wins ahead of tile 10, though single profiles of it and its variants spread from 198.7 to 209.9.

## Why the prediction was wrong

The path was named rightly: paddings behind a late table2, a hole of some 4 us, a clock near 0.6 after it, 3.90 us a tile. Its sizes were not, and with them the sign went: the forecast was for a net of -2.8 us and the profile has +4.5. **The step that failed** is the time of the padding, and with it of the first tile behind all sends. I had pad_i at 131.4 us and from it layer1:9 3.2 us earlier than before (147.9 against 151.07); measured are 135.95 and 153.28, 2.2 later. That is 5.4 of the 7.3 us by which the profiles miss the forecast, and kernel 1, which moves only the tables' entries, gets some 4 of them back. The rest is the clock, the tile stage and the tail, each mis-sized by 0.4 to 0.9. By the signs that I had set, the steps with sums fail too: two of the five take over 4.5 us (4.54 and 4.98). The sizes, in the order of my sum:

- **First send 57.3: measured 58.80.** The sum of VectorE's work was right (56.73 in kernel 1, at full clock). I had read VectorE at 8 or 9 in every slice from 2 to 14 of [rows 1]; one of them is a 5, which changes no term. The sum left out that TensorE may run at half clock from 39 to 46 us and that VectorE's resid:2 stands behind it: +1.5. The rival of ScalarE was not it: lgc:0 ended at 53.8, and top2:0 stood behind VectorE's own work. Kernel 3 shows that it would have been next.
- **Tile 0 loaded at 101.6: measured 104.06.** norm2:7 ends near 101.9, not 98.5: 1.5 is the first send's; the rest is VectorE waiting 0.39 and 1.50 us, the second for mult:7 behind a table load at 88.60. What releases the load is the doubling of group 7 behind norm2:7 (101.93, load 2.13 later; the same 2.13 in kernels 1 and 2), where I had the 32nd send and its 3.1 us as the last wait.
- **Last send 139.4: measured 142.03.** 1.5 is the first send's; and the hole ahead of the 33rd send, which I had nearly gone, still has 1.66 us. A load behind it alone could be issued at 145.1 to 146.6 (an estimate: 3.1 us behind it as before, 4.55 as in kernel 1), so the padding decided (148.48).
- **Layer1:0 5.0 us behind its load: measured 6.0.** Tile 0's row turn (108.70) stands on TensorE behind rank:5 and the last routers.
- **tx:7 24.2 us behind layer1:0: measured 25.0.** pad_i stood at 135.95, not 131.4: 4.5 late. From there on the step was right: tile 9 loaded 12.53 us behind pad_i, 12.6 predicted.
- **layer1:9 at 147.9: measured 153.28** (start in the chain). 4.5 from pad_i; the rest is the second pass, which I priced at 0.42 inside layer1's 1.73. The twelve places did their part: tile 10's load is issued 1.15 us behind tile 9's. But at tile 9 TensorE has only one bank for both turns, so that tile 10's turn waits for two passes (0.54, and 0.72 from start to start), 1.45 us.
- **Clock 1.8: measured 2.2 to 2.4** for 3.6 us of standing still.
- **Tile stage +0.3: measured +0.9.** The second pass alone costs 3.2 (kernel 2), so without it the stage would be 2.3 shorter than before. Kernel 8, which has the sums' new steps but not the rest, is at +0.84 (one profile, another chip): so the sums' places would explain the 0.9, and the w2 copy that left VectorE and the second pass that came would cancel. VectorE's copy is 543 ns, not 422, there are two, and `ty` waits for them by the shared bank.
- **Tail -1.65: measured -0.74.** Layer2:38 ends 0.6 earlier (0.8 predicted), halves give 0.1 (0.4), two queues about 0.0 (0.45): from the first of the last loads to VectorE's first sum of them it takes 2.77 us against 2.56, to the end 7.84 against 8.01. From the last layer to the end it is 13.5 us, not 12.9. The old tail in this kernel costs 1.1 (kernel 15), where the last six scatters follow each other without a wait (305.70 to 312.65).
- **Warm-up at zero: right.** gates:0 takes 2.05 us with it and without. By the Trainium skill (TensorE: Matmul & The Clock Gate, Part 1) activity ahead should release the half rate; the eleven small matmuls of before did not show it.
- **The price of a table switch**: 1.28 us again in the rows after, not the 2.66 that the Trainium skill states (ScalarE: Activation LUTs, What ACT_TABLE_LOAD costs).

The third rival (two-pass copy and later table eat the lead) named what happened, with too low a price: 287 to 288.8, because it took the late table alone to cost one tile, and added to it neither the half clock of the start nor the second pass. It had a chance of 0.15.

## What to carry over

A gain early in a chain is only real if the thing that is *next* late was costed with its own queue: here one late entry of VectorE's list, with eight issues and a landing behind it, turned 0.6 us of earlier sends into 2.8 us of later load, and the stillness that follows (3.6 us) costs TensorE two thirds of itself again in clock (2.2 to 2.4). Moving the table's entries forward by a tile gave 4 us back on chip one; on two others the changed kernel isn't slower, and no such gain shows (kernels 9, 12 to 14). An operation counted as hidden "beside layer1" must also be looked up in the waits of its bank: TensorE's next turn, not the layer, was waiting for it. And work taken off one engine's critical wait can return as a queue on another (VectorE's lag became GpSimd's scatters).

## What was not expected of the hardware

- The half clock moves from one execution to the next at the same instructions: in 39 to 46 us the granted clock is 0.57, 0.62, 0.76 to 0.79 or 1.00 in kernels that have the same lists up to there, and the first send then starts between 56.4 and 59.2 us, at 56.4 and 56.7 where it is 1.00 without a filler. After a long stillness of TensorE ahead of a tile's row turn the half clock came each time, on every chip: after 3.60 us and more the next layer1 took 3.3 to 3.6 us, after 1.20 its usual 1.89 (kernel 6).
- A VectorE copy of 128x256 float32 out of PSUM takes 543 ns with a scale and a bias from SBUF as per-partition values, 422 without.
- Chips differ by 14 to 15% in this kernel (289.8 against 330.8 to 332.3 us for the kernel before), with stops of 2 to 12 us on all engines between 60 and 190 us, and the change's ratio by 3%.
